# Strassen's seven products for a batch's fc1, with split weights kept in memory and streamed

## What is computed

```python
h = gelu(x @ fc1_w.T + fc1_b)                       # 4 x 1024 x 2048
y = concat([h @ fc2_w.T + fc2_b, h @ experts_w[e[b]].T + experts_b[e[b]]], -1)
x = x + y
attn_in = tanh(x @ W1 + b1); scores = attn_in @ v
mask = prefix, postfix or all-but-self, by type of the batch
p = softmax(where(mask, scores, -1e30)); pooled = p @ x / count(mask)
x = x + pooled
```

## Time and profile before

| | |
|---|---|
| median of 3 runs | 852.8 us (851.95 to 853.72) |
| profiled execution | 853.88 us, of which the span from first to last instruction is 851.9 |
| PE busy | 829.3 us, 97% of the span, 3736 matmuls and transposes |
| DVE, ACT, POOL busy | 49%, 47%, 10% |
| granted TensorE clock | 0.98 of full speed on average |
| DMA | 31.4 MB, mean 37 GB/s |

### The profile page before, as it was taken

How to read it: one execution, slowest core, us unless ns; L and a number is a source line. 1 busy time by engine, 2 the same in 40 slices (tenths; PEclk the granted TensorE clock), 3 DMA queues, 4 the chain that set the end, 5 groups by cost and what they waited for, 6 DMA issues and landing times.

```text
span 851.9 us, 10976 instructions
## 1 busy us (share of the span) xinstructions
PE 829.3 (97%) x3736; PEld 679.7 (80%) x3736; DVE 421.2 (49%) x733; ACT 403.7 (47%) x681; POOL 85.3 (10%) x133
## 2 busy tenths in 40 slices
PE   7999999999999999999999999999999999999866
PEld 5888888888788888888888888888878888888655
DVE  4343554337554474435565356433745446443564
ACT  6454455445465354444548235544545634454321
POOL 2300000002001400003000220000200041000250
PEclk9999999999999999999999999999999999999967
DMA  8610000010000210001000120000100022000002
GB/s 289 230 38 1 0 13 13 14 56 7 1 1 13 75 64 12 13 13 64 1 1 1 41 107 13 13 13 14 50 1 1 1 74 74 13 13 13 13 1 98
DMA packets 24318, 31.36 MB, mean 37 GB/s; under 512 B 2368, under 2 KB 14672, under 8 KB 23888
## 3 DMA queue, kind: packets, MB, share of 16 engines
q1 hardware_dynamic: 24112, 30.68, 10.6%
q0 software_dynamic: 160, 0.01, 0.0%
HBM read 22.30 MB, written 8.39 MB: 36 GB/s over the span
## 4 chain that ended last, share of the span: by engine, by line
PE 96%; DVE 2%; ACT 1%; DMA 0%; issue 0%; SPq 0%; DVEq 0%; ACTq 0%
PE h L453 14%; PE y L453 14%; PE h L454 14%; PE h L455 14%; PE y L454 14%; PE y L455 14%; PE j L453 2%; PE j L455 2%; PE j L454 2%; PE j L490 1%; PE j L521 1%; PE j L522 1%; PE j L515 1%; PE j L503 1%; PE j L539 1%; DMA w1T<-in_fc_w 0%
## 5 line engine op out<-in xcount | busy, mean ns | idle before, releaser
L656 DVE TENSOR_TENSOR hl<-g,hh 128x512 fp32r<-128x512 f32 x128 | 88.6, 692 | 335.0 <-ACT hh L564 335.0
L632 ACT ACTIVATE g<-h,bcol 128x512 f32<-128x512 f32 x128 | 88.1, 689 | 343.3 <-PE h L455 343.2
L453 PE MATMUL h<-xh,w1h 128*128 128x512 f32 x512 | 202.3, 395 | 6.0 <-DVE w1l L656 6.0
L453 PE MATMUL y<-hh,w2h 128*128 128x512 f32 x512 | 204.2, 399 | 0.1
L454 PE MATMUL y<-hl,w2h 128*128 128x512 f32 x512 | 200.7, 392 | 0.0
L455 PE MATMUL y<-hh,w2l 128*128 128x512 f32 x512 | 200.5, 392 | 0.0
L455 PE MATMUL h<-xh,w1l 128*128 128x512 f32 x512 | 200.0, 391 | 0.0
L454 PE MATMUL h<-xl,w1h 128*128 128x512 f32 x512 | 200.0, 391 | 0.0
L453 PEld LDWEIGHTS h<-xh,w1h 128*128 128x128 f32 x512 | 96.6, 189 | 26.4 <-issue 6.5
L453 PEld LDWEIGHTS y<-hh,w2h 128*128 128x128 f32 x512 | 96.8, 189 | 22.2 <-issue 1.5
L455 PEld LDWEIGHTS y<-hh,w2l 128*128 128x128 f32 x512 | 96.9, 189 | 20.8
(11 more groups left out here) (160 smaller groups left out, 628.2 us busy)
## 6 DMA issues: line engine op xcount, KB each, us to landing
raw<-in_x SPq DMA_DIRECT2D x36, 256.0 KB, 3.7
out_x<-x1T SPq DMA_DIRECT2D x24, 256.0 KB, 2.0
w2T<-in_experts_w SPq DMA_DIRECT2D x19, 256.0 KB, 3.2
w1T<-in_fc_w SPq DMA_DIRECT2D x3, 1024.0 KB, 10.9
w2T<-in_fc_w SPq DMA_DIRECT2D x3, 768.0 KB, 12.1
out_x<-w1T SPq DMA_DIRECT2D x8, 256.0 KB, 2.0
w1T<-in_fc_w SPq DMA_DIRECT2D x2, 256.0 KB, 3.9
w1T<-in_fc_w SPq DMA_DIRECT2D x1, 512.0 KB, 5.0
```

The source lines that it names most:

```text
L453: nc.tensor.matmul(ps, ah, bh, start=first, stop=False)
L632: nc.scalar.activation(g[:, ring, :], hb[ring][:, :], ACT.Gelu, bias=bcol[:, R_FC1 + s:R_FC1 + s + 1]).then_inc(gelu_done, 1)
L656: return nc.vector.tensor_tensor(out_, in_, hi_.bitcast(f32), ALU.subtract)
```

## The change

fc1 is done for a whole batch (both halves of 512 tokens, columns of B) and two hidden tiles at a time (rows of A) as one 2 x 2 block product by the Winograd form of Strassen's scheme: A11 to A22 are w1 blocks (hidden tile x half of the features), B11 to B22 x blocks (half of the features x half of the tokens), S1 to S4 and T1 to T4 sums and differences of them. Seven products of 2 k-tiles x 3 = 6 matmuls replace eight.

- A batch is now a **first part** of 8 **steps** p = 0 to 7 (`step`), each with the seven products for hidden tiles 2p and 2p+1, between which lie the fc2 matmuls of two earlier units (a unit is one hidden tile of one half; groups 0 to 7 are its output tiles), and a **second part** of 16 units u with fc2 alone, for the other half of the tokens, whose hidden values wait in the new buffer `hst`.
- Products share two PSUM banks, `hA` (P1, P6, P7, P4) and `hF` (P5, P3, P2). The products that go on in a bank start from what stands in it, so ACT first copies partial sums out (`snap`, three per step) and DVE adds a bank to a copy (`add`, three per step); then come four gelus.
- x: the 7 blocks x 2 k-tiles are split once per batch (`xc` tasks, u = 0 to 12); POOL makes the T sums from four raw tiles `xr`, which SP loads in two rounds, at u = 0 and u = 5. The residual is loaded again into `x1T` (`load_residual`), so `x1` is one addition less.
- Weights: in the first batch w1 blocks (with S sums, by POOL), w2 and the experts are split and written to memory (`w1s`, `w2s`, `exs`). From then on SP streams the split blocks: `load_w1` in four groups per step, each when its last product is done, `load_w2` per unit into a ring of three. The next batch's expert is split in steps 0 to 3 (`ex`).
- The tasks of the second layer are placed anew: `expE` and both halves of `expPW` stand together at the end of step 4, `ysum` of the first half at u = 1, just ahead of the unit that needs the banks.

The core of the diff:

```diff
+PAIRS = HC // 2
+KH = DC // 2
+P1, P5, P6, P3, P7, P2, P4 = range(7)
+W_OF = {P1: A11, P5: S1, P6: S2, P3: S4, P7: S3, P2: A12, P4: A22}
+X_OF = {P1: B11, P5: T1, P6: T2, P3: B22, P7: T3, P2: B21, P4: T4}
+IN_A = (P1, P6, P7, P4)
+W_GROUPS = [(0, 1, P1), (4, 7, P3), (1, 2, P2), (2, 4, P4)]
+X_SPLITS = [B11, B21, B22, T1, T3, T2, T4]
+X_TILE = {B11: 0, B21: 2, B22: 3, T1: 0, T3: 1, T2: 3, T4: 2}
-    return {6: ([("stats",)], []), 8: ([("bc", 0)], [("bc", 1)]), 9: ([], [("expE",), ("expPW", 0)]),
-            10: ([("sums",), ("expPW", 1)], [("sums1",)]), 11: ([("den", 0, CH)], []),
+          (4, 2): [("expE",), ("expPW", 0), ("expPW", 1)], (5, 0): [("sums",), ("sums1",)],
+POST_U = {1: [("ysum", oc) for oc in range(OC)], 2: [("x1", 0), ("x1", 1)], 3: [("x1", 2), ("x1", 3)], 4: [("attn",)],
+          5: [("xn", 0)], 6: [("xn", 1)], 7: [("xn", 2)], 8: [("xn", 3)], 9: [("score",)]}
+PREP_U = {0: [0, 1], 1: [2], 2: [3], 3: [4], 4: [5], 5: [6], 7: [7, 8], 8: [9], 9: [10], 10: [11], 11: [12], 12: [13]}
...
+            def product(kind, b, p, i):
+                bank, w, x_, g = hA if i in IN_A else hF, W_OF[i], X_OF[i], GROUP_OF[i]
+                if kind == "first":
+                    pe.wait_ge(w1lo, 4 * p + g + 1)
+                else:
+                    pe.wait_ge(w1_in[g], b * (16 * PAIRS) + 16 * (p + 1 - PAIRS))
+                if i == P1:
+                    wait(pe, gelu_done, steps(b, p, 4, 0))
+                elif i == P5:
+                    wait(pe, add_done, steps(b, p, 3, 0))
+                elif i in (P6, P3, P7):
+                    pe.wait_ge(snap_done, steps(b, p, 3, {P6: 1, P3: 2, P7: 3}[i]))
+                else:
+                    pe.wait_ge(add_done, steps(b, p, 3, {P2: 1, P4: 2}[i]))
...
+                product(kind, b, p, P1)
+                product(kind, b, p, P5)
+                group(0)
+                product(kind, b, p, P6)
+                group(1)
+                jobs(0)
+                product(kind, b, p, P3)
+                group(2)
+                product(kind, b, p, P7)
+                group(3)
+                jobs(1)
+                product(kind, b, p, P2)
+                group(4)
+                product(kind, b, p, P4)
+                for i in (5, 6, 7):
+                    group(i)
+                jobs(2)
...
+                snap(kind, b, p, P1)
+                snap(kind, b, p, P5)
+                if weights:
+                    split_w1(p + 1, 0)
+                if kind == "first":
+                    split_w2(2 * p)
+                snap(kind, b, p, P6)
+                tasks(0)
+                if weights:
+                    split_w1(p + 1, 1)
...
+                gelu(b, p, 1)
+                gelu(b, p, 2)
+                if kind == "first":
+                    split_w2(2 * p + 1)
+                tasks(1)
+                gelu(b, p, 3)
+                split_h(b, 2 * p)
...
+                gelu(b, p, 4)
+                split_h(b, 2 * p + 1)
...
+                if p == PAIRS - 1:
+                    for oc in range(OC):
+                        gate(sp, out_put[oc], b * (16 * CH // OUTS))
+                        load_residual(b, 0, oc)
...
+                        load_x(b, 0)
```

914 lines of the change are left out of this document (636 added, 278 removed).

## The result

The changed kernel takes 940.1 us (median of 4 runs, 934.5 to 949.9), the kernel before 853.3: a ratio of 1.0997 [1.0944, 1.105]. The prediction was 874, in a range of 842 to 890. The direction was right, the size was not: +87 us where +21 was expected. Single launches, here the one of 949.9 us, were slow ones, and the ratios leave them out.

What follows compares the result with a forecast made beforehand. PE's matmul stream, 97% busy at 226.7 ns each, was taken as the bound. Against 853.9 us, -43.5 + 19.6 + 2 + 4.4 + 3 x 7.9 + 3 x 4.9 gave 874.8, forecast as 874, range 842 to 890.

Steps and rivals of the forecast that it cites:

- 192 matmuls fewer: In fc1, a step's products take 42 matmuls where 48 stood: 192 fewer in all, worth -43.5 us.
- The exp stall: At step 5 of each loop batch, PE waits 3.7 us for ACT's copy behind the exponentials; +4.9 with clock.
- The ysum term: At unit 16, ysum waits for x: stalls of 3.4 us (first batch) and 6.2 (others), floor 2.2; +4.4 and +7.9.
- by bytes ... after a start at U+1.7: After step 7's end (U), 2.36 MB take 7.4 us from U+1.7, so x block B21 lands about U+9.0.
- the residual goes out a step earlier, B21 lands at U+6.2: First batch, U being step 7's end: x block B21 lands 6.2 us after it, so the stall is 3.4 us.
- the rest: Other steps and loop loads: PE has cover, loads average 200 GB/s, w1 asked for 9 us ahead; no cost.
- The sentence on P4's end: At P4's end 9 matmuls cover one gelu of 0.69 us; ACT 1.4 us late there would cost 32 times.
- The head: Before step 1, splits and sums on DVE and ACT delay its P1 to 35.6 us; +19.6 with clock.
- The clock: PE's lower clock after waits: 1.7 us for head and each long ysum stall, 1.0 first batch's, 1.2 each exp.
- rival A: Faster: at unit 16 x lands in time, stalls are 2.2 us and the clock holds; 842 us, chance 0.24.
- The stream of the first batch: First batch's steps: splitting, writing and rereading weights moves 4.7 MB per step; +2 us in all, of 0 to 12.
- rival B: Head and first batch hang on DMA: 890 to 895 us, chance 0.10; sign: its steps 1 to 7 over 16 us.

Runs made afterwards that it cites:

- a: Changed kernel with the first two x splits of the next batch moved behind ysum; 909.6 us, 1.0616 of the kernel before.
- b: Changed kernel with the first four x loads issued at the start of step 5, in the loop batches only; 906.5 us, 1.0593 of the kernel before.
- (c): Changed kernel with the second round of x loads two units later (u = 7) and their splits following; 915.9 us, 1.0733 of the kernel before.
- (f): Changed kernel with the next expert's weight split moved behind the last gelu of the step; 922.9 us, 1.0773 of the kernel before.
- (j): (i) plus x splits and GpSimd's sums in later units, and the identity tile made ahead of the first sums; 854.1 us, 0.9992 of the kernel before.
- (i): g plus later expert split and earlier ysum (868.5 us), then the first batch's w1 reloads moved behind the third unit's w2 load; 860.2 us.
- g: Changed kernel with x splits behind ysum, earlier first x loads, later second x round, exponentials in two pieces and reordered head; 877.5 us, 1.0283 of before.

## Why the prediction was wrong, point by point

**What held.** 192 matmuls fewer at an unchanged pitch. That ysum becomes the longest wait, at unit 16, behind x that lands late, with a floor of 2.2 us (2.1 to 2.3 in a and b). The exp stall, 3.7 predicted and 3.48 measured three times. The sign.

**The ysum term was mis-sized** (3.4 + 3 x 6.2 = 22.0 us of stall; measured 40.5). The issue order and SP's pitch were right. For the three loop batches (28.9 us in place of 18.6) the step that failed is "by bytes ... after a start at U+1.7": it took the DMA engines as idle before, and they were full from 364 on; B21 landed at U+11.3 and not at U+9.0. The 2.6 us from landing to ysum left out GpSimd's sum, which costs 1.1. For the first batch (11.6 in place of 3.4, nearly half of the miss) it is "the residual goes out a step earlier, B21 lands at U+6.2": the residual did, but the four w1 reloads of 1.5 MB behind it were left out of the count, and B21 landed at U+12.5. They are in the kernel's SyncE program, at the end of `first_step`.

**The streamed w2 was dismissed** (the rest: "w1 groups asked for 9 us ahead", nothing for w2; measured 17.2). The average of 200 GB/s was right (189 on the page). But a queue in order passes on each stop of its head, and the gated x loads at unit 5 held three w2 loads. (c) shows what the place of these loads costs: 14 us of waits and 24 of time. I had asked what queues behind SP's gates on output rows, not behind its gates on x tiles.

**The gelus** (nothing beyond the head; measured 12.6). The sentence on P4's end, "if ACT came 1.4 us late there", named the place and not the cause, which was there to read in the diff: the expert split stands between the second and third gelu on ACT and ahead of the third's addition on VectorE. The prediction walked through it in the head alone. In steps 1 to 3 of the first batch it costs 1.03 us each by VectorE's order, in two later batches 2.56 and 2.00 by the late landing. (f) shows it: all five are gone.

**The head** (35.6; measured 39.13). The order worked out was right row by row until DVE's sums of T4, which took 1.21 us each beside GpSimd: P6 began at 25.16 and not at 22.3, 2.9 of the 3.5 us. PE was also not started at 5.98 but at 10.0: GpSimd makes the identity tile, on which it waits, behind its first sums. In (j) the first matmul comes at 6.47, but the next waits move into its place: step 1 begins at 34.26, in (i) at 34.24.

**The clock** (1.7 x 4 + 1.0 + 3 x 1.2 = 11.4; measured 28.9 by the clock rows, 34.7 if PE's busy time is compared). Laid out by place, the loss is 9.7 us behind the four ysum waits (6.1 taken), 6.1 behind the three exp stalls (3.6) and 3.3 in the head (1.7): 2.4, 2.0 and 3.3 each, so these prices were too low by 7.7 in all. The larger part of the miss is gaps that the prediction did not have: 7.3 behind w2 waits and 1.6 behind a gelu's. The half clock behind `den` adds 1.7 to what the kernel before has, and the tail gives 0.8 back. "PE kept 1.0 through every busy stretch", said for rival A, is not so: the kernel before ran at 0.50 with PE busy throughout from 466 to 472 and from 670 to 676, which its page of 40 slices does not show.

**The stream of the first batch** (2 us) is not seen. Steps 1 to 3 took 17.9, 16.3 and 16.3 us, steps 4 to 7 15.1 to 15.2, against 15.0: 3.1 of the excess is the gelus' waits, 1.5 half clock at the start of step 1, and PE never waits for a weight there. So the sign given for rival B, steps of over 16 us, came up in three steps for a cause that is not B's. Rival B is not what happened: the head was 3.5 us late and not 6.4, and most of the loss is in the loop.

In all, the span grew by 85.5 us where 20.9 was summed up, 64.6 more: 18.5 ysum, 17.2 w2, 7.6 the gelus behind the head, 17.5 the clock, 5.8 of the matmuls' saving that did not show, 0.8 the idle time of the head, less 0.7 for exp and the 2 of the first batch's stream. (The head's 3.5 us are not added once more: most of what is above 0.8 is clock, in the 17.5.)

## What to carry to other kernels

A large saving on the bound engine only counts for what its feeders leave of it: here the same matmuls took 940 or 854 us by nothing but the place of loads, splits, sums and exponentials. Walk each in-order queue at the place where the work changes its kind, and for every instruction that can wait ask what stands behind it, and how full the DMA engines are *before* it. Waits add up fairly well (g gave 63 us where the parts promised 78), but each one removed uncovers a smaller one: five moves gave the first 63 us, five more the last 23.
